# Edge attention of a four-layer graph network: the turning of the probabilities, three DMA transposes per half against one

## What is computed

```python
node_att = jax.nn.softmax(x @ node_w, axis=0)
h = x @ edge_w
e = h @ h.T
e = jnp.where(adj > 0, e, NEG_BIG)
edge_att = jax.nn.softmax(e, axis=1)
combined_att = node_att * edge_att
support = x @ weight
output = adj * combined_att @ support
return output + bias
```

## Time and profile before

| | us |
|---|---|
| median of 3 runs | 2943.82 |
| lowest and highest run | 2940.87, 2946.68 |
| the profiled execution, its own time | 2943.13 |
| its span in the trace | 2941.3 |
| PE busy | 2752.5 (94%) |
| DVE, ACT busy | 1862.5 (63%), 1553.4 (53%) |
| edge attention, about | from 2070 to 2634 of the span |
| DMA transposes (L923) | 132, median 1.23 to 1.27 of SP's time each |

### The profile page before, as it was taken

One profiled execution on the slowest core, in us unless ns is written; L12 is line 12 of the kernel. 1 busy time (PEld: TensorE's weight loads), 2 busy tenths in 40 slices (PEclk: granted clock), 3 DMA queues, 4 the chain that ended last, 5 costly groups with the idle time before them and its releaser, 6 DMA issues. The chain is left out here.

```text
span 2941.3 us, 64010 instructions
## 1 busy us (share of the span) xinstructions
PE 2752.5 (94%) x23308; PEld 1788.8 (61%) x23308; DVE 1862.5 (63%) x3387; ACT 1553.4 (53%) x2376; POOL 392.8 (13%) x372
## 2 busy tenths in 40 slices
PE   8989999989989998989899799979899999979998
PEld 6667676767767776767676444457444444434443
DVE  4479897988879798988897322245444555633222
ACT  4467786867768687767687222222343334324222
POOL 0001111111111111111111012300111111210222
PEclk9999999999999999999999899989999999989999
DMA  4221111111111111111110345531455667743454
GB/s 157 81 80 39 39 38 39 38 39 51 48 53 39 39 38 39 38 39 39 44 48 5 129 145 203 198 110 46 115 140 148 185 177 190 201 116 113 172 209 145
DMA packets 220379, 280.58 MB, mean 95 GB/s; under 512 B 138721, under 2 KB 157153, under 8 KB 208865
## 3 DMA queue, kind: packets, MB, share of 16 engines
q1 hardware_dynamic: 220128, 277.13, 30.3%
HBM read 195.39 MB, written 38.44 MB: 79 GB/s over the span
## 5 line engine op out<-in xcount | busy, mean ns | idle before, releaser
L760 DVE SCALAR_TENSOR_TENSOR att_pt_low<-att_ps_t,att_pt_high 128x512 f16<-128x512 f32 (+1 forms) x1056 | 633.5, 641 | 102.0 <-ACT att_pt_high L729 85.8
L729 ACT ACTIVATE att_pt_high<-att_ps_t 128x512 f16<-128x512 f32 (+1 forms) x1056 | 538.6, 559 | 288.6 <-PE att_ps_t L661 286.7
L661 PE MATMUL att_ps_t<-all_ident,att_scores 128*128 128x128 f32 (+1 forms) x3872 | 539.5, 280 | 73.8 <-issue 67.5
L767 DVE CUSTOM_DVE_ANT_0 att_scores<-att_slots,att_adj 128x1024 f32<-128x1024 f32 x528 | 574.2, 1088 | 12.0 <-PE att_slots L673 11.5
L735 ACT ACTIVATE att_scores<-att_scores,att_nmax 128x1024 f32<-128x1024 f32 x528 | 553.8, 1049 | 11.0 <-DVE att_nmax L773 11.0
L673 PE MATMUL att_slots<-l_kk,att_q 128*128 128x512 f16 x2112 | 498.4, 359 | 7.0 <-DMA att_q<-att_q_raw 5.6
L661 PEld LDWEIGHTS att_ps_t<-all_ident,att_scores 128*128 128x128 f32 (+1 forms) x3872 | 410.2, 139 | 110.8 <-issue 74.6
L1276 PE MATMUL a_ps<-l_y,a_adj 128*128 128x512 f16 (+1 forms) x1936 | 431.2, 382 | 9.0 <-DVE a_adj L1290 4.7
L643 PE MATMUL att_ps_pv<-l_vv,att_pt_high 128*128 128x129 f16 (+1 forms) x3872 | 433.6, 221 | 0.4 <-DVE att_pt_low L760 0.4
L643 PE MATMUL att_ps_pv<-l_vv,att_pt_low 128*128 128x65 f16 (+1 forms) x3872 | 403.6, 193 | 0.0
L643 PEld LDWEIGHTS att_ps_pv<-l_vv,att_pt_high 128*128 128x128 f16 (+1 forms) x3872 | 351.6, 98 | 63.5 <-issue 2.5
(11 more groups left out here) (140 smaller groups left out, 2938.9 us busy)
## 6 DMA issues: line engine op xcount, KB each, us to landing
l_adj<-in_adj_cols SPq DMA_DIRECT2D x44, 1408.0 KB, 6.1
att_adj<-in_adj SPq DMA_DIRECT2D x22, 1354.0 KB, 6.0
l_adj_tiles<-in_adj SPq DMA_DIRECT2D x22, 1354.0 KB, 5.9
p_x_in<-x SPq DMA_DIRECT2D x66, 256.0 KB, 2.6
att_q<-att_q_raw SPq DMA_DIRECT2D x88, 128.0 KB, 2.3
a_xres<-x SPq DMA_DIRECT2D x44, 256.0 KB, 2.7
scores_rows<-edge_raw SPq DMA_DIRECT2D x8, 842.0 KB, 3.4
p_x_in<-in_x SPq DMA_DIRECT2D x22, 256.0 KB, 2.6
```

The source lines that it names most:

```text
L661: mm = nc.tensor.transpose(ps_t[0:r, g % 2, (k % GB) * P:(k % GB + 1) * P], sp_sb[:, h % 2, k * P:k * P + r], ident[:, :])
L729: nc.scalar.activation(pt[0][:, g, 0:w], ps_t[:, g % 2, 0:w], ACT.Copy, scale=P_S) \
L760: nc.vector.scalar_tensor_tensor(out=pt[1][:, g, 0:w], in0=ps_t[:, g % 2, 0:w], scalar=P_S, in1=pt[0][:, g, 0:w], op0=ALU.mult, op1=ALU.su ...
L767: nc.vector.tensor_tensor_reduce(out=sp_sb[:, h % 2, lo:lo + width], in0=slots[:, (NC * h + c) % 2, 0:width], in1=adj[:, u, lo:lo + width] ...
```

## The change

`turn` issues one transpose for all 22 blocks of a half in place of three of 8, 8 and 6 blocks, two per tile in place of six. `used` and `pt_turned` no longer count chunks but whole tiles, so the first transpose of tile t waits until all products of tile t-1 are done, each transpose waits for all three chunks of its half, and the products of tile t wait for both transposes whole. Nothing else differs; the number of instructions on PE, DVE and ACT is the same.

```diff
-        pt_turned = [s.sem(f"pt_turned{c}") for c in range(NC)]
+        pt_turned = s.sem("pt_turned")
...
                 t = 2 * m + u
-                for c in range(NC):
-                    k = keys_of(c)
-                    if not is_tile(m, u, 0):
-                        wait_apart(sp, used, NC * (t - 1) + c + 1, pad_clear)
-                    for a, made in enumerate((part_high, part_low)):
-                        wait_apart(sp, made, NC * t + c + 1, pad_clear)
-                        sp.dma_start_transpose(pt[a][:, k, :], part[a][:, k.start * P:k.stop * P]) \
-                            .then_inc(pt_turned[c], 16)
+                if not is_tile(m, u, 0):
+                    wait_apart(sp, used, t, pad_clear)
+                for a, made in enumerate((part_high, part_low)):
+                    wait_apart(sp, made, NC * (t + 1), pad_clear)
+                    sp.dma_start_transpose(pt[a][:, :, :], part[a][:, :]).then_inc(pt_turned, 16)
...
                 t = 2 * m + u
-                for c in range(NC):
-                    pe.wait_ge(pt_turned[c], 32 * (t + 1))
-                    if c == 0 and not (isinstance(m, int) and m == 0):
-                        pe.wait_ge(r_ready, t - 1)
-                    for k in range(*keys_of(c).indices(T)):
-                        r = rows_of(k)
-                        for a, b in ((0, 0), (0, 1), (1, 0)):
-                            mm = nc.tensor.matmul(ps_o[:, u, :], pt[a][0:r, k, :], sup[b][0:r, k, :],
-                                                  start=k == 0 and a + b == 0, stop=k == T - 1 and a == 1)
-                    mm.then_inc(used, 1)
+                pe.wait_ge(pt_turned, 32 * (t + 1))
+                if not (isinstance(m, int) and m == 0):
+                    pe.wait_ge(r_ready, t - 1)
+                for k in range(T):
+                    r = rows_of(k)
+                    for a, b in ((0, 0), (0, 1), (1, 0)):
+                        mm = nc.tensor.matmul(ps_o[:, u, :], pt[a][0:r, k, :], sup[b][0:r, k, :],
+                                              start=k == 0 and a + b == 0, stop=k == T - 1 and a == 1)
+                mm.then_inc(used, 1)
...
                 if not is_tile(m, u, 0):
-                    for c in range(NC):
-                        act.wait_ge(pt_turned[c], 32 * t)
+                    act.wait_ge(pt_turned, 32 * t)
...
-                if not is_tile(m, u, 0):
-                    dve.wait_ge(pt_turned[c], 32 * t)
+                if c == 0 and not is_tile(m, u, 0):
+                    dve.wait_ge(pt_turned, 32 * t)
...
-                dve.wait_ge(used, NC * (t + 1))
+                dve.wait_ge(used, t + 1)
```

More of the change, by code:

```diff
@@ L878, in copies @@
             return (2 * t, CT + t, 3 * CT)[band]
-        def keys_of(c):
-            return slice(c * CT, min((c + 1) * CT, T))
         @block.sync
```

## The result

| | before | changed |
|---|---|---|
| median | 2945.25 us (4 runs) | 2967.26 us (4 runs, 2964.29 to 2974.69) |
| ratio | | 1.0082, 95% interval 1.0069 to 1.0094 |
| the profiled execution, its span | 2941.3 | 2962.5 |
| stretch S | 526.2 us | 552.3 us |

What follows compares the result with a forecast made beforehand. PE, busy 94% of the span, sets the pace. Band 2 14.4, last tile 9.2 and clock 2 sum to 25.6 us on 2943.1, that is 2968.7; the median 0.7 above gives 2969 us, range 2958 to 2989.

Steps and rivals of the forecast that it cites:

- S: From first products of edge attention to first load of the next stage; the forecast sum was 25.6 us more.
- bands 0 and 1: Scores between products last 13.9 and 9.2 us and cover X of 9.0 us: no cost.
- signs that I had listed under "Wrong": Signs against it: issue rows of several us, waits in band 1, clock 0.5 in band 2, no PE waits.
- X: Time for the merged pair of transposes, from first issue until both have landed: 9.0 us, bounds 8.6 to 10.2.
- band 2, without the clock: Six gaps between products, each 6.6 us against X of 9.0, leave 2.4 us open each: 14.4 us.
- last tile: No further scores cover the merged pair before the last products: 9.2 us (8.8 to 10.4).
- clock: Last products start at a granted clock of 0.50 after PE's idle gap: 2 us (1.5 to 2.5).
- 1.85 us there leaves the clock at 1.00, so I cost them at nothing: In band 2 PE's waits grow to about 2.4 us without a fall of the clock: no cost.
- the full fall in every gap as a rival: Clock falls in each band 2 gap: up to 3.4 us lost six times, 20 us, 2989 us; chance 0.15.
- The rival of the late second half: Long issue holds SP, so the second half starts with a hole: X = 10.2, 2986 us; chance 0.13.
- The fast transfer: Long transpose runs at a copy's 412 GB/s: X = 5.3, last tile costs 5.5 us, 2949 us; chance 0.08.
- The waits behind the transposes: Loads queued behind the transposes, such as mirror and adjacency, sit behind 5 us more of transposes: hidden, no cost.

Runs made afterwards that it cites:

- experiment 7: Changed kernel plus unread products where PE waits for transposes, 8 per band 2 tile and 38 before the last products: 2964.31 us, ratio 1.0080.
- experiment 5: Changed kernel with two turned buffers per half in place of one: 2952.21 us, ratio 1.0031.
- experiment 8: Kernel before, with the last block of keys in edge attention's products multiplied over 128 rows where it had 20: 2939.14 us, ratio 0.9988.
- experiment 9: Kernel before, with 128 rows in place of 20 in edge attention and in the second and fourth layers' adjacency products: 2932.68 us, ratio 0.9964.
- experiment 4: Changed kernel, but PE multiplies with the high half first and waits for the low half only before the last 22 products: 2956.72 us, ratio 1.0048.
- experiment 1: Kernel before with six short transposes that wait for all products of the tile before, and products that wait for all six: 2988.77 us, ratio 1.0162.
- experiment 2: Kernel before, but only the transposes wait for the whole tile before; products still wait chunk by chunk: 2951.44 us, ratio 1.0029.
- experiment 3: Kernel before, but only the products wait for all six transposes; transposes still start chunk by chunk: 2952.20 us, ratio 1.0032.

## Why the prediction was right

The direction, the place and the sum held: PE waits for the low half in band 2 and at the end, and nowhere in bands 0 and 1. In band 2 there are five such waits of 1.6 to 2.1 us, 9.9 in all, where six of 2 to 3 were named. Two of the signs that I had listed under "Wrong" came too, issue rows of several us and a clock of 0.5 in band 2; both are taken up below. By S:

| term | forecast | measured |
|---|---|---|
| X, first issue to start of products | 9.0 | 8.6 to 8.8 |
| bands 0 and 1 | 0 | 0 |
| band 2, without the clock | 14.4 | 12.9 |
| last tile | 9.2 | 8.7 |
| clock | 2 | 4.9 (4.6 by experiment 7) |
| behind the last products | 0 | -0.4 |
| S | 25.6 | 26.1 |

**X** came out near its lower bound of 8.6: the pause between the halves, which I kept in the point estimate, does not exist. That makes six gaps and the last one 0.3 us shorter each than forecast, 2 us in all. The six periods of band 2 are 144.0 us where they were 127.7, 16.3 more. Of these 3.4 are the clock: two sets of products take 16.13 in place of 14.44 us. The other 12.9 are the gaps, 2.15 each. A third fall of the clock, from 2533.0 for 3.4 us, slows scores and is nearly free: PE was to wait for the transposes in that gap anyway. It is why the sixth gap has no wait of its own.

**The step that failed is "1.85 us there leaves the clock at 1.00, so I cost them at nothing".** In the changed kernel the clock was at 0.50 in three of the six tiles, after waits of about 2 us, and in three kernels without a wait for transposes in band 2 after one for DVE, of 2.22 us in experiment 5 and of 2.00 and 2.01 in experiments 8 and 9. In experiment 4 the wait of 2.21 us left it up, in the changed kernel 2.02 and 2.13, in experiment 1 even 2.91 and 3.40. No wait up to 1.86 us in band 2 was followed by a fall. So in this stage it can go either way from 2 us of waiting on, up to 3.4, and a wait that is lengthened from 1.5 to 2 us can cost 1.7 us more. What decides it between two equal waits isn't shown. That term, 2 us in my sum for the last tile alone, is 4.9 by the lengths of the slow stretches (half of 3.4 twice and of 3.1 once) and 4.6 by experiment 7. I had the full fall in every gap as a rival, at 3.4 us each; it came in three of six, and cost 1.7 us in two of them. The row of the first layer that it went by is no clean case, for within the 6.8 us PE was busy 2.68 us only the earlier trace rows. The right total owes something to luck: X was too high by 2.0 us in all, the clock too low by 2.9. And the 2969 was meant for the whole time, of which only S follows the sum; the profiled spans differ by 21.2 us in place of 25.6, by the shifts outside S that no term covers.

**The rival of the late second half** had its premise right and its result wrong. The long issue does hold SP as long as its half's bytes last, 3.4 us, and the second issue stands 3.5 us behind the first, not 1.4 as I wrote under what would show it. From 1.21 and 1.24 us for 6 and 8 blocks I read that the size hardly counts; between 8 and 22 blocks it does. But no hole opens, since SP issues the second while the first still moves: 212 GB/s without a break.

**The fast transfer** did not happen: 212 GB/s, as the earlier trace rows had it. The Trainium skill, "DMA: Bandwidth & Descriptors", "Latency and other measured facts", gives 261 GB/s for a transpose with a non-contiguous middle dimension and 350 to 400 for a contiguous one. The rows here stay below both, a fifth below the first, for 8 blocks (213) and for 22 (212).

**The waits behind the transposes** were hidden as counted. None of PE's waits in S in the changed kernel ends on the mirror or the adjacency; the mirror issued at 2511.36 landed 9.4 us later.

The rule to coalesce of the Trainium skill, "DMA: Bandwidth & Descriptors", "Rules for kernel authors", is borne out in its own terms: with both waits in place two long transposes take 8.7 us where six short ones take 9.7, because six issues stand 1.4 us apart. It is outweighed by what merging does to the waits.

## What to carry to other kernels

A transfer that is merged takes its neighbours' semaphores with it. Before merging, write down for the first and last byte when the destination is free and when the reader needs it; with one buffer, merging both sides puts the full length of the transfer between two uses, and it must fit into what the reader does in between. Short transfers with one side kept in pieces (experiments 2 and 3) took away 19 to 20 of the 26 us here. If it must be merged, order the reader's work so that it starts with the half that lands first (13 us), or add a buffer (16 us). And look at the end of a pipeline, where there is no cover: one tile of 22 made 10 of the 26 us.

## What was not expected of the hardware

- A DMA transpose of 22 blocks mostly holds SP, the engine that issues it, for 3.2 to 3.5 us (single ones 3.8 and 4.1), one of 6 or 8 blocks for 1.2. A long one could delay what stands behind it in the same queue; here nothing there was urgent.
- The granted clock fell to 0.50 after single waits of 2.0 to 2.2 us in the middle of a stage that is busy otherwise, but not in all cases; it stayed up after some of 2.9 and 3.4. Useless matmuls in the wait kept it up (experiment 7).
- PE stands about 0.1 us when a matmul's weights change from 128 to 20 rows, and again on the way back. In the trace of before the last product with 128 rows starts at 2503.07, the first with 20 at 2503.38, 0.31 us later where one with 128 rows follows after 0.21 or 0.22; the scores after the last one with 20 rows start 0.31 later too. Together it is 0.21 us per tile in experiments 4 and 8. A zero-padded full block is cheaper here than a short one, worth 0.36% (0.22 to 0.49) in this kernel.
